# One of three first-layer parts of a CIN in three float32r passes instead of float32

## The reference

```python
emb = tables[feat_idx, sparse]                      # (2048, 26, 32)
x0 = emb; xk = emb
for w, bb in ((conv1_w, conv1_b), (conv2_w, conv2_b)):
    hp = einsum('bhd,bmd->bhmd', xk, x0).reshape(-1, h * 26, 32)
    xn = sigmoid(einsum('oi,bid->bod', w, hp) + bb)  # 128 outputs
    xk = xn[:, :64]; res.append(xn[:, 64:])
cin_out = concat(res).sum(-1) @ cin_w + cin_b
deep_out = tanh MLP 845 -> 1024 -> 512 -> 256 -> 1   # on emb and dense
return linear_out + cin_out + deep_out + bias
```

## Time and profile before

| | us |
|---|---|
| median of 3 runs (1583.1 to 1590.08) | 1586.48 |
| the profiled execution | 1593.15 |
| its span, first to last instruction | 1591.3 |
| granted TensorE clock, mean over the span | 0.995 |
| TensorE busy | 1515.7 (95%), 6552 matmuls |
| VectorE busy | 1152.5 (72%) |
| ScalarE busy | 646.6 (41%) |
| GpSimd busy | 686.5 (43%) |

### The profile page before, as it was taken

How to read it: one execution, slowest core, us unless ns; L and a number is a source line. 1 busy time by engine, 2 the same in 40 slices (tenths; PEclk the granted TensorE clock), 3 DMA queues, 4 the chain that set the end, 5 groups by cost and what they waited for, 6 DMA issues and landing times.

```text
span 1591.3 us, 23672 instructions
## 1 busy us (share of the span) xinstructions
PE 1515.7 (95%) x6552; PEld 661.8 (42%) x6552; DVE 1152.5 (72%) x1113; ACT 646.6 (41%) x904; POOL 686.5 (43%) x600
## 2 busy tenths in 40 slices
PE   0599999999999999999999999999999999999999
PEld 0233333333333333333333333333333337787876
DVE  3278788888888888878787888888888685344442
ACT  2344344443444444344434344444443323444443
POOL 7538574637464655546454646374731110000000
PEclk9999999999999999999999999999999999999999
DMA  6688788988899888989998989998999983846741
GB/s 132 136 217 214 204 220 230 218 232 210 233 202 236 217 235 208 239 202 241 192 237 205 245 205 236 217 242 211 238 220 233 223 226 96 196 125 167 176 127 53
DMA packets 177869, 322.08 MB, mean 202 GB/s; under 512 B 30160, under 2 KB 106032, under 8 KB 177796
## 3 DMA queue, kind: packets, MB, share of 16 engines
q1 hardware_dynamic: 140989, 294.37, 72.0%
q10 hardware_dynamic: 23534, 20.23, 5.7%
q0 software_dynamic: 13312, 7.06, 4.7%
HBM read 300.24 MB, written 21.31 MB: 202 GB/s over the span
## 4 chain that ended last, share of the span: by engine, by line
PE 82%; DMA 5%; SPq 3%; DVE 3%; POOL 3%; issue 3%; ACT 1%; ACTq 0%; DVEq 0%; POOLq 0%
PE acc L834 39%; PE acc L828 19%; PE bc L971 14%; PE bc L814 5%; DMA xb<-x_rows 3%; PE bc L821 3%; POOL emb L604 3%; SPq L511 2%; DVE xb L781 2%; SPq L522 1%; DMA emb<-table,idx_stage 1%; DVE hp L781 1%; PE bc L806 1%; DMA x_halves<-deep_halves 0%; ACT sq L1013 0%
## 5 line engine op out<-in xcount | busy, mean ns | idle before, releaser
L604 POOL DMA_INDIRECT emb<-table,idx_stage x416 | 484.4, 1164 | 319.0 <-DVE hp L781 161.7
L781 DVE TENSOR_TENSOR hp<-bc,xk 128x1024 f32<-128x1024 f32 x384 | 446.2, 1217 | 215.5 <-PE bc L814 180.6
L781 DVE TENSOR_TENSOR xb<-xb,xk 128x1024 f32<-128x1024 f32 x448 | 570.9, 1329 | 20.1 <-DMA xb<-x_rows 19.9
L834 PE MATMUL acc<-xb,w2s 128*64 128x512 f32 x1792 | 410.5, 595 | 3.1 <-DVE xb L781 2.6
L834 PE MATMUL acc<-hp,w2s 128*64 128x512 f32 x1536 | 360.4, 604 | 0.0
L828 PE MATMUL acc<-sq,w1s 128*128 128x512 f32 x768 | 351.4, 607 | 2.9 <-ACT sq L1013 2.2
L1013 ACT ACTIVATE sq<-bc 128x1024 f32<-128x1024 f32 x192 | 182.9, 1027 | 231.0 <-PE bc L821 231.0
L834 PEld LDWEIGHTS acc<-xb,w2s 128*64 128x64 f32 x1792 | 126.4, 137 | 258.9 <-issue 218.2
L615 POOL TENSOR_TENSOR r<-r 128x512 f32<-128x512 f32 x96 | 134.0, 1395 | 220.9 <-ACT r L1020 114.2
L828 PEld LDWEIGHTS acc<-sq,w1s 128*128 128x128 f32 x768 | 142.1, 192 | 182.7 <-issue 181.2
L834 PEld LDWEIGHTS acc<-hp,w2s 128*64 128x64 f32 x1536 | 99.2, 137 | 195.3 <-issue 168.0
(11 more groups left out here) (61 smaller groups left out, 812.7 us busy)
## 6 DMA issues: line engine op xcount, KB each, us to landing
xb<-x_rows SPq DMA_DIRECT2D x448, 256.0 KB, 6.0
xb<-x_rows SPq DMA_DIRECT2D x192, 512.0 KB, 4.9
w_raw<-W SPq DMA_DIRECT2D x48, 512.0 KB, 3.6
xb<-x_rows SPq DMA_DIRECT2D x128, 128.0 KB
x0t<-x_halves ACTq DMA_DIRECT2D x252, 52.0 KB
x_full<-x_halves SPq DMA_DIRECT2D x96, 128.0 KB
emb<-table,idx_stage POOLq DMA_INDIRECT x416, 4.3
x_halves<-deep_halves SPq DMA_DIRECT2D x16, 384.0 KB, 6.1
```

The costliest lines, as they stand in the source:

```text
L604: nc.gpsimd.indirect_dma_start(out=emb[:, m, :], out_offset=None, in_=table, in_offset=bass.IndirectOffsetOnAxis(ap=idx_stage[:, m:m + 1], ...
L781: nc.vector.tensor_tensor(product(n)[:, :], x[:, :], xk[sl % 2][:, :], ALU.mult).then_inc(multiplied, 1)
L834: last = nc.tensor.matmul(acc_y[H * c:H * c + H, :], w2s[:, ORDER[n], :], src[:, c * CHUNK:(c + 1) * CHUNK], start=(n == 0), stop=(n == PA ...
```

## The change

Part 0 of the first layer is no longer one float32 matmul but three float32r passes per chunk: weights high x squares high, weights low x squares high, weights high x squares low. ScalarE squares slot 0 twice (once into `sq[0]`, once rounded into `sq_hi[0]`), and VectorE subtracts the two into `sq_lo[0]`. It does this for step s+1 between products 8 and 9 of step s. Parts 1 and 2 stay in float32. In chunk 0 the three passes come first, in chunk 1 last. The weights' halves are made once, in the prologue.

Beside this it puts seven idle float32 matmuls (`keep_busy`) into the prologue before the wait for `x0_loaded` and three before the first fill 0 of step 0; it moves some of the first tile's gathers (of the embeddings of tiles 1 and 2) to other products; it spreads the 34 `load_x` DMAs evenly over the eight steps of the last two tiles, last step included (before: about 2 in each step of the last tile but one, then about 8 in each of three steps); and `orow` becomes `h_raw[0]`.

```diff
+HALVED = 1
-                    if ahead == 1:
-                        if sl == 0:
-                            sp.wait_ge(dense_dumped, 64)
-                        load_x(0, sl, 4 * STEPS)
-                    if ahead == 0 and sl < STEPS - 1:
-                        load_x(0, 1 + sl, STEPS)
+                    if ahead == 1 and sl == 0:
+                        sp.wait_ge(dense_dumped, 64)
+                    if ahead < 2 and not is_first:
+                        load_x(0, (1 - ahead) * STEPS + sl, 2 * STEPS)
...
-                    gather_in(s, range(14, M), (0, 1, 2, 3, 4, 4, 4, 4, 5, 6, 7, 8))
+                    gather_in(s, range(12, 24), (0, 0, 0, 1, 2, 3, 4, 4, 4, 4, 5, 6))
+                    gather_in(s, range(24, M), (7, 8))
...
+                    gather_in(s + 1, range(4), (7, 8, 10, 12))
                     add_up(t, 1, r2, r2_step, y2_read, 1, sum2)
-                    gather_in(s + 2, range(5), (1, 2, 3, 4, 6))
+                    gather_in(s + 2, range(4, 9), (1, 2, 3, 4, 6))
                     add_up(t, 3, r1, r1_step, xn_read, 2, sum1)
-                    gather_in(s + 2, range(5, 11), range(7, PAIRS))
+                    gather_in(s + 2, range(9, 15), range(7, PAIRS))
                     add_up(t, 2, r2, r2_step, y2_read, 1, sum2)
-                    gather_in(s + 3, range(11, 22), (0, 1, 1, 2, 3, 3, 4, 5, 6, 7, 7))
+                    gather_in(s + 3, range(15, 22), range(7))
...
+            def lower_squares(s):
+                for k in range(HALVED):
+                    dve.wait_ge(sq_full, halved_by(s, k))
+                    dve.wait_ge(squared, squared_by(s, k))
+                    nc.vector.tensor_tensor(sq_lo[k][:, :], sq[k][:, :], sq_hi[k][:, :], ALU.subtract).then_inc(sq_low, 1)
...
+            dve.wait_ge(w1_high, 1)
+            nc.vector.tensor_tensor(w1_lo[:, :, :], w1s[:, 0:HALVED, :], w1_hi[:, :, :], ALU.subtract).then_inc(w1_low, 1)
...
+            lower_squares(-1)
+            lower_squares(0)
...
+                        if n == 9 and not (ahead == 0 and sl >= STEPS - 2):
+                            lower_squares(s + 1)
                         nc.vector.tensor_tensor(product(n)[:, :], x[:, :], xk[sl % 2][:, :], ALU.mult).then_inc(multiplied, 1)
...
-            def contract_k(c, acc_k):
+            def contract_k(c, acc_k, s):
                 cols = slice(c * CHUNK, (c + 1) * CHUNK)
-                for k in range(K1):
-                    last = nc.tensor.matmul(acc_k[:, :], w1s[:, k, :], sq[k][:, cols], start=(k == 0), stop=(k == K1 - 1))
+                halved = [(w[:, k, :], sq_hi[k][:, cols]) for k in range(HALVED) for w in (w1_hi, w1_lo)]
+                halved += [(w1_hi[:, k, :], sq_lo[k][:, cols]) for k in range(HALVED)]
+                full = [(w1s[:, k, :], sq[k][:, cols]) for k in range(HALVED, K1)]
+                passes = halved + full if c == 0 else full + halved
+                for i, (w, x) in enumerate(passes):
+                    if c == 0 and i == 2 * HALVED:
+                        pe.wait_ge(sq_low, halved_by(s, HALVED - 1))
+                    last = nc.tensor.matmul(acc_k[:, :], w, x, start=(i == 0), stop=(i == len(passes) - 1))
...
+            def keep_busy(n, acc_free):
+                for _ in range(n):
+                    nc.tensor.matmul(acc_free[:, :], idf[0:ND, :], dense_rows[:, 0:CHUNK], start=True, stop=True)
+
+            keep_busy(7, acc[0])
...
+                        if start and kind == "fill" and what[0] == 0:
+
+                            pe.wait_ge(xn_read, 2)
+                            keep_busy(3, acc[1])
...
             def square(k, slot):
-                nc.scalar.activation(sq[k][:, :], bc[slot][:, :], ACT.Square).then_inc(squared, 1)
+                if k < HALVED:
+                    nc.scalar.activation(sq[k][:, :], bc[slot][:, :], ACT.Square).then_inc(sq_full, 1)
+                    nc.scalar.activation(sq_hi[k][:, :], bc[slot][:, :], ACT.Square).then_inc(squared, 1)
+                else:
+                    nc.scalar.activation(sq[k][:, :], bc[slot][:, :], ACT.Square).then_inc(squared, 1)
```

More of the change, by code:

```diff
@@ L216, in build @@
         bias_out = sb("bias_out", [P, 1])
-        orow = sb("orow", [P, CHUNK])
         bias1 = sb("bias1", [P, 1])
@@ L246, in build @@
         sq = [sc(f"sq{k}", [P, COLS]) for k in range(K1)]
+        sq_lo = [sc(f"sq_lo{k}", [P, COLS], F32R) for k in range(HALVED)]
+        sq_hi = [sc(f"sq_hi{k}", [P, COLS], F32R) for k in range(HALVED)]
+        w1_hi = sc("w1_hi", [P, HALVED, P], F32R)
+        w1_lo = sc("w1_lo", [P, HALVED, P], F32R)
         hp = [sc(f"hp{i}", [P, COLS]) for i in range(len(BY_PE))]
@@ L264, in build @@
         h_raw = [sb(f"h_raw{i}", [P, CHUNK]) for i in range(2)]
+        orow = h_raw[0]
         h_hi = sb("h_hi", [P, HIDDEN, CHUNK], F32R)
@@ L310, in build @@
         squared = sem("squared")
+        sq_full = sem("sq_full")
+        sq_low = sem("sq_low")
+        w1_high = sem("w1_high")
+        w1_low = sem("w1_low")
         multiplied = sem("multiplied")
@@ L344, in squared_by, with halved_by @@
             return s * K1 + (K1 + k + 1)
+        def halved_by(s, k):
+            return s * HALVED + (HALVED + k + 1)
         def multiplied_by(s, n):
@@ L645, in tile @@
                     free_emb(t, DEEP_N)
-                    gather(range(8), gathered)
-                    for m, (signal, count) in enumerate(((k_contracted, 1), (xk_made, 1), (xk_made, 2), (squared, K1 + 1),
-                                                         (squared, K1 + 2), (squared, 2 * K1))):
+                    gather(range(6), gathered)
+                    gather(range(6, 8), gathered)
+                    for m, (signal, count) in enumerate(((k_contracted, 1), (xk_made, 1), (xk_made, 2), (squared, K1 + 1))):
                         pool.wait_ge(signal, count)
@@ L871, in _ @@
             pe.wait_ge(sel_rounded, 2)
+            pe.wait_ge(deep_loaded, DEEP_LOADED)
+            def keep_busy(n, acc_free):
+                for _ in range(n):
+                    nc.tensor.matmul(acc_free[:, :], idf[0:ND, :], dense_rows[:, 0:CHUNK], start=True, stop=True)
+            keep_busy(7, acc[0])
             pe.wait_ge(x0_loaded[0], 16 * ROW_LOADS)
@@ L875, in _ @@
                 spread_sum(k, k, x0t[0])
-            pe.wait_ge(w1_step, W1_STEPS)
+            pe.wait_ge(w1_low, 1)
             pe.wait_ge(squared, K1)
             for c in range(2):
-                contract_k(c, first_acc(-1, c))
+                contract_k(c, first_acc(-1, c), -1)
             pe.wait_ge(w2_loaded, W2_LOADED)
@@ L929, in tile @@
                                 pe.wait_ge(y2_read, s)
-                            contract_k(what, first_acc(sl, what))
+                            contract_k(what, first_acc(sl, what), s)
                         elif kind == "terms":
@@ L1029, in _ @@
                 turned_deep(i, i)
+                if i == 0:
+                    act.wait_ge(w1_step, W1_STEPS)
+                    nc.scalar.activation(w1_hi[:, :, :], w1s[:, 0:HALVED, :], ACT.Copy).then_inc(w1_high, 1)
             act.wait_ge(first_halves, FIRST_HALVES)
```

## The result

The changed kernel takes 1648.12 us (4 runs, 1643.99 to 1648.71) where the kernel before takes 1587.91 (4 runs; the 3 known before the prediction had 1586.48): **1.0376 times as long, 95% interval 1.0342 to 1.041**. The forecast was 1622 (1603 to 1645), and slower with a chance of 0.9. The direction and the ring of the steps held; the size didn't: +60.2 us for +35.6, by terms outside the ring. The profiled execution is 1647.68 us, its span 1645.9.

What follows compares the result with a forecast made beforehand. TensorE's own work was taken to bound the CIN stage. The terms, mainly +42.6 us from a 20.2 us ring over steps 6 to 61, summed to +35.6; on 1586.5 that gave 1622 us, range 1603 to 1645.

Steps and rivals of the forecast that it cites:

- the ring: CIN steps: K fill, two squares, low half, products 9 to 12, last contraction, fill 0; period 20.2 us against 19.02.
- What bounds the kernel; shares and places: CIN stage: TensorE's own work sets the pace; VectorE has room by share, but its free time lies before product 0.
- Three passes, 0.35 us a step: TensorE, part 0 in both chunks: three float32r passes replace each float32 matmul, gaining 0.35 us a step.
- the 1 us for `load_x`: Last eight steps: 1 us added for spread load_x DMAs behind late xb loads on SP's queue; bounds 0 and 5.
- The step with the transposes: One step in four, with the embeddings' transposes: 20.2 us here too, against 20.1.
- The prologue, -2.5 us: Up to step 1's K fill: idle matmuls fill the wait, a contraction runs at full speed; 81.28 to 78.8.
- The first tile's own steps, 103.2: Steps 1 to 5: 22.4 plus four of 20.2, against 105.5 before; moved gathers end step 5's stall; -2.3 us.
- the ring collects more: Rival, CIN steps: GpSimd's sums delay the low half and products 9 to 12, TensorE gaps add; 1640 to 1680, 10%.
- never by a bit: Low half on VectorE: by the skill, either free or put off by a whole GpSimd sum.
- The last stretch, 42.3: Behind step 62's K fill: no ring as the low half is skipped, stall and slow stretch gone; -3.2 us.
- nothing in the sum hangs on that part: Final sum: the profiled execution's 6.7 us above the runs' median was subtracted as not affecting the terms.
- the deep stage: After the CIN steps: nothing changes, 270.5 us before and in the forecast.

## Why the prediction was right or wrong

- **What bounds the kernel; shares and places.** Right. VectorE had room for its new instruction (after product 12 it costs nothing) and not at that place.
- **Three passes, 0.35 us a step.** Right: from fill 0 to the next K fill 10.78 us for 11.12, and 18.69 for 19.03 where nothing else decides. In the step with the transposes it is 0.26 (19.83 for 20.09).
- **The ring, 20.2 us a step.** Right in the three links that were tried: a product, the low half and a square. Steps 6 to 61 came within 0.1 us of the sum, and that is in part luck: the plain ring was 0.1 us shorter than 20.25, two steps of a tile 0.1 and 0.2 longer, the 1 us for `load_x` never came (the last steps took 20.2), and two steps of 20.5 and 21.2 took its place.
- **The step with the transposes.** Right, 20.11.
- **The prologue, -2.5 us: wrong, +2.75.** I had the seven idle matmuls fill the wait for the rows from HBM and let a contraction behind them run at full speed. They ran at the slow one throughout (12.31 us) and delayed the first K fill by 3 us (51.01 to 53.97), and the contraction behind them was 0.7 us faster for the 2.2 I had given it. Without any side edit the K fill of step 1 comes at 81.79. The bounds of 0 and -5 left out a loss, though one could have been seen: the prediction itself reads the contractions of rows 9 as half at twice the usual spacing, and 14 records at twice 0.45 us are 12.5 us, where TensorE's wait for the rows, from 42.1 to 51.0 in the trace of the kernel before, is 9.
- **The first tile's own steps, 103.2: wrong, 113.9.** The largest miss, and the step of the prediction that failed most. I gave the moved gathers their gain in step 5 and nothing for what the same edit does in step 1: gathers that went out on ScalarE's squares now wait for VectorE's first product, the transposes wait 6.42 us behind them (0.76 in the kernel before), and TensorE's clock falls meanwhile, which is 1.4 us more. Undoing the edit gave 7.7 us back, and the gain in step 5 was not the edit's in this kernel, since the stall is gone without it. In the kernel before, the same gates make the transposes wait 2.01 us only; what makes it 6.42 beside the passes is open.
- **The rival "the ring collects more".** The measured 1648 lies in its range (1640 to 1680), but not by its mechanism, which came true in small. In step 3 GpSimd's sums stretched the low half to 2.04 us and the four products to 5.41, and the step took 22.0 us; step 2 took 21.2, with products 3 and 4 stretched to 3.43 beside a GpSimd sum. In steady steps one in four is longer by 0.19: GpSimd's last sum starts just before the low half. One more is longer by 0.11, because ScalarE's first square starts at K+0.65 for K+0.53.

VectorE and GpSimd in step 3 of the changed kernel:

```profile
137.82 2.04 DVE L754 TENSOR_TENSOR sq_lo<-sq,sq_hi 128x1024 fp32r<-128x1024 f32 x1 [2.40 <-ACT sq_hi L1061]
139.79 5.41 DVE L808 TENSOR_TENSOR xb<-xb,xk 128x1024 f32<-128x1024 f32 x4
...
137.49 1.28 POOL L627 TENSOR_TENSOR r<-r 128x512 f32<-128x512 f32 x1
138.85 1.60 POOL L630 TENSOR_TENSOR r<-r 128x256 f32<-128x256 f32 x1
140.53 1.32 POOL L632 TENSOR_TENSOR sum<-r 128x128 f32<-128x128 f32 x1
```

and in the steady step from K = 622.10:

```profile
624.61 1.42 DVE L754 TENSOR_TENSOR sq_lo<-sq,sq_hi 128x1024 fp32r<-128x1024 f32 x1 [2.26 <-ACT sq_hi L1061]
...
624.49 0.46 POOL L632 TENSOR_TENSOR sum<-r 128x128 f32 x1 [0.19 <-POOL r L630]
```

The Trainium skill (SBUF — State Buffer, "two separate sides") has a VectorE instruction with two SBUF inputs and a GpSimd operation that reads SBUF exclude each other for a whole instruction. The rows agree: the low half is 0.8 us over its usual 1.22, and the sum next to it 1.60 for 0.73; both times the low half ends 1.1 us after the sum that was already running (138.77 to 139.86, 624.95 to 626.03). So what it is put off by is what is left of a running sum, 0.19 us in the steady step, and the prediction's "never by a bit" was wrong.

- **`load_x`.** The stall at the end went, but not by the spread: it goes with the ring, whose step is long enough for the burst, and alone the spread wins nothing.
- **The last stretch, 42.3: 43.8.** I wrote that the low half is skipped behind the K fill of step 62. It isn't: that K fill is the last, its low half is made (the 64th), and the ring closed once more (fill 0 at K+9.4).
- **The median.** I subtracted the 6.7 us by which the profiled execution lay above the median. The changed kernel's lies on its median (1647.68 and 1648.12), and so the 6.7 us are missing in the forecast. That "nothing in the sum hangs on that part" was wrong: the profile of before held late `xb` loads (VectorE idle 19.9 us for them, 0 to 1.1 in the five profiles of kernels with the whole ring), and these stalls sat in the 1088.6 us from which the term of the steps was taken. That they are the 6.7 us is likely and not shown.

Together: 5.2 + 10.7 + 0.1 + 1.5 + 1.4 = 18.9 us in the profiled execution. The forecast of 1622.1 was missed by 26.0: these 18.9, 6.7 for the offset, and 0.4 by which the median lies above the profiled execution. Against +60.2, which is taken from the new median of before (1587.91), the offset is 5.2 instead of 6.7, and the miss 24.6. The 1.4 us of the deep stage did not come again on the second chip.

## What to carry to other kernels

An engine with free time can still lack it where an instruction is put: draw the chain from what the instruction waits for, through what is queued behind it, to what that releases, and add it up to a period. If it is above the bound engine's own, every link costs its full length (three were tried here), down to that engine's own period, and a cure is to move the instruction to where its engine waits anyway, here four products later, which takes the ratio from 1.0376 to 1.0027. Cost the side edits of a change with the same care as its core: here idle matmuls and moved gates, both meant to help, cost 11.6 us beside the passes and some 4 each alone. And a stall that disappears beside a slower step was perhaps hidden by it, not mended.

## What the hardware showed that I had not expected

- Seven idle float32 matmuls on 13 rows (14 records), back to back for 12.31 us, took 0.88 us a record and 1.76 a matmul, twice the 5.35/12 = 0.45 us a record of a steady step. The profile's clock reads 1.00 in that stretch all the same, but the trace has no record of the granted clock before 61.7 us, so this 1.00 says nothing. At 61.8 us, inside the contraction behind them, the spacing of the records falls from 0.85 to 0.43 us. From there on clock and spacing agree:

```profile
61.80:68.50 6.70, 5.42 (x19) 2.61 (x18) 0.00 (x0) 5.22 (x8) 2.84 (x3) 1.00 0.81 178
68.60:75.30 6.70, 6.70 (x15) 3.15 (x14) 4.20 (x4) 2.55 (x3) 2.28 (x2) 0.50 0.21 29
```

The three idle matmuls that start at 67.40 are 0.43 to 0.54 us a record apart at first and 0.86 from 69.0 on. So their 13 rows don't make them slow; the clock does. And the seven did not bring the full clock forward: its first record, 1.00, begins at 61.7 us with them, at 60.8 without them and at 59.3 in the kernel before.
- The `xb` loads come late in some executions, for several steps at a time, and VectorE stands up to 4.2 us before a product. Kernels whose steps are shorter than the ring's show it (VectorE idle for them 5 to 27 us in all), the five profiles with the whole ring hardly do (0 to 1.1). The runs of the faster kernels scatter more (1572 to 1592 on the chip where the changed kernel's were 1645 to 1650). The late loads are a likely reason; but the fastest of them, 1571.89 us, has 18.4 us of such idle time, so not all of it costs.
